# Startup order of a four-layer GNN kernel: table additions first, table parts and weight split inside the first step, statistics behind the last message, three idle products

## What is computed

```python
def _gine_layer(x, src, dst, edge_attr, eps, We, be, W1, b1, gamma, beta, W2, b2):
    e = edge_attr @ We + be                       # edge_attr: one weight w per edge
    m = jax.nn.relu(x[src] + e)
    agg = jax.ops.segment_sum(m, dst, num_segments=x.shape[0])
    h = ((1.0 + eps) * x + agg) @ W1 + b1
    mu = jnp.mean(h, axis=0)
    var = jnp.mean(jnp.square(h - mu), axis=0)
    h = (h - mu) * jax.lax.rsqrt(var + BN_EPS) * gamma + beta
    h = jax.nn.relu(h)
    return jax.nn.relu(h @ W2 + b2)
...
x = _layernorm(x + x_after_four_layers)
```

## Time and profile before

| what | value |
|---|---|
| median of 3 runs | 1656.23 us (1652.46 to 1661.26) |
| profiled execution, its own time | 1657.55 us |
| span of its trace, first to last instruction | 1655.7 us |
| mean granted TensorE clock | 0.968 of full speed |
| gathers of layer 0 from the table | 272, from 32.95 to 371.57 us |
| first gather of layer 1 | 427.21 us |

### The profile page before, as it was taken

One profiled execution on the slowest core, in us unless ns is written; L12 is line 12 of the kernel. 1 busy time (PEld: TensorE's weight loads), 2 busy tenths in 40 slices (PEclk: granted clock), 3 DMA queues, 4 the chain that ended last, 5 costly groups with the idle time before them and its releaser, 6 DMA issues. The chain is left out here.

```text
span 1655.7 us, 20783 instructions
## 1 busy us (share of the span) xinstructions
PE 1413.6 (85%) x8107; PEld 856.7 (52%) x8107; DVE 1278.7 (77%) x2059; ACT 283.3 (17%) x669; POOL 1081.9 (65%) x1149
## 2 busy tenths in 40 slices
PE   4798888889788889888968888888897888899888
PEld 3364555555444555555535555555544555565563
DVE  7997888875677878787567887787667877787867
ACT  3011111116100100111610100110170100110014
POOL 6777777770577777776067777777507777777740
PEclk9999999999899999999989999999998999999999
DMA  8777777771677777777177777777617777777743
GB/s 315 218 212 211 211 211 211 211 236 54 198 210 210 211 211 211 212 210 224 57 220 212 210 210 211 211 209 211 188 69 238 210 212 211 210 210 210 211 157 127
DMA packets 109194, 330.66 MB, mean 200 GB/s; under 512 B 20794, under 2 KB 21946, under 8 KB 109092
## 3 DMA queue, kind: packets, MB, share of 16 engines
q0 software_dynamic: 91200, 298.92, 62.1%
q1 hardware_dynamic: 17892, 30.36, 5.4%
HBM read 316.40 MB, written 12.80 MB: 199 GB/s over the span
## 5 line engine op out<-in xcount | busy, mean ns | idle before, releaser
L457 POOL DMA_INDIRECT rows<-node_table,src_all x1124 | 1062.6, 945 | 508.0 <-issue 395.8
L879 DVE SCALAR_TENSOR_TENSOR rows<-We_ps,negw_all,rows 128x512 f32<-128x512 f32 x1140 | 778.4, 743 | 283.2 <-DMA rows<-node_table,src_all 281.3
L1229 PE MATMUL y_ps<-table_parts,src_onehot 128*128 128x512 f32 x2240 | 630.8, 425 | 22.1 <-DVE src_onehot L782 22.1
L1229 PEld LDWEIGHTS y_ps<-table_parts,src_onehot 128*128 128x128 f32 x2240 | 421.3, 199 | 268.0 <-issue 165.6
L1187 PE MATMUL pair_ps<-rows,onehot 128*32 128x512 f32 x2504 | 347.8, 622 | 202.9 <-DVE rows L879 202.5
L1187 PEld LDWEIGHTS pair_ps<-rows,onehot 128*32 128x32 f32 x2504 | 51.5, 108 | 327.7 <-DVE rows L879 214.6
L782 DVE TENSOR_TENSOR src_onehot<-y_ps,src_bc 128x1280 fp32r<-128x1280 f32 x112 | 165.7, 1482 | 1.2 <-issue 1.2
L571 ACT COPY pair_sb<-pair_ps 128x512 f32<-128x512 f32 x80 | 47.0, 587 | 655.8 <-PE pair_ps L1187 655.8
L1278 PEld LDWEIGHTS h_ps<-uT,W_sb 128*128 128x128 f32 x1184 | 136.4, 193 | 31.3 <-issue 31.0
L1278 PE MATMUL h_ps<-uT,W_sb 128*128 128x128 f32 x1184 | 143.5, 279 | 0.0
L1332 PE MATMUL y_ps<-rows,hT 128*128 128x512 f32 x288 | 124.6, 593 | 1.5 <-ACT hT L652 1.5
(11 more groups left out here) (118 smaller groups left out, 646.2 us busy)
## 6 DMA issues: line engine op xcount, KB each, us to landing
rows<-node_table,src_all POOLq DMA_INDIRECT x1124, 3.7
node_table<-rows SPq DMA_DIRECT2D x29, 256.0 KB
x_now<-x_pad SPq DMA_DIRECT2D x10, 512.0 KB, 7.7
W_sb<-W SPq DMA_DIRECT2D x4, 1024.0 KB, 5.5
rows<-W SPq DMA_DIRECT2D x4, 1024.0 KB, 8.4
out<-rows SPq DMA_DIRECT2D x8, 256.0 KB
node_table<-rows SPq DMA_DIRECT2D x8, 224.0 KB
be_bc<-be SPq DMA_DIRECT2D x5, 256.0 KB, 7.9
```

The lines of the kernel that those rows point to most:

```text
L457: nc.gpsimd.indirect_dma_start(rows[:, slot, :], None, source, bass.IndirectOffsetOnAxis(places[:, t:t + 1], 0)).then_inc(landed[q], 16)
L879: last = nc.vector.scalar_tensor_tensor(rows[:, slot, :], We_of, negw_all[:, t:t + 1], row, ALU.mult, ALU.max)
L1229: last = nc.tensor.matmul(y_ps[k % 2][:, :], src_onehot[:, k % 2, b, :], table_parts[:, part, b, :], start=(part, b) == PRODUCTS[0], stop= ...
```

## The change

- VectorE's ten additions of be (L851) stand directly behind `negw_all`. The split of the weights, the one-hots and placement of block 0 and the ten `lo_part` stand behind the messages of quad 0 of layer 0's first step; the first two source one-hots behind quads 1 and 2; `keep_w(0)` behind quad 3.
- ScalarE copies the weight parts and sums of block 0 inside the first step. TensorE makes all eight spreads of source indices ahead of the layers, sums the weights behind quad 0 and places them in quad 1, and the forty products of the first two gathered tiles begin at place 0 and not before the first step.
- The columns of source indices are stored by tile and parity of the block: seven small copies for five.
- In a layer's last step the eight statistics instructions stand behind quad 7, not behind quad 6.
- `GAP`, the number of idle products at each of the two places at a layer's end, is 3 for 4.

POOL's instructions and waits are as they were, and SP's too.

```diff
-    GAP = 4
+    GAP = 3
...
-        shares, done = {}, -2
+        shares, done = {}, -2 if l else -1
...
             for m in range(3):
                 keep_spread(m)
-            act.wait_ge(w_parts_ready, 1)
-            move_parts(0, 0)
-            move_parts(0, 1)
             for k in range(BLOCKS):
                 act.wait_ge(staged, k + 1)
                 hi_part(k)
-                if k == 1:
-                    copy_w(0)
-                elif k + 2 < SPREADS:
-                    keep_spread(k + 2 + (k == 0))
+                if k + 3 < SPREADS:
+                    keep_spread(k + 3)
...
+                        else:
+                            act.wait_ge(w_parts_ready, 1)
+                            move_parts(0, 0)
+                            move_parts(0, 1)
+                            copy_w(0)
...
-            for m, q in enumerate(pe_quads(L - 1, 0)):
-                tile = FULL[q][-1][1]
-                nc.vector.tensor_copy(src_cols[:, m:3 * (BLOCKS - 1):3], src_all[:, tile:T - LAST:STEP])
-            for m, q in enumerate(pe_quads(L - 1, BLOCKS - 1)):
-                t, k = STEP * (BLOCKS - 1) + FINAL[q][-1][1], 3 * (BLOCKS - 1) + m
-                nc.vector.tensor_copy(src_cols[:, k:k + 1], src_all[:, t:t + 1])
+            for _, group in itertools.groupby(BY_TILE, key=lambda place: place[:2]):
+                (tile, _, i, q), steps = (places := list(group))[0], len(places)
+                k, t = COLUMNS[i, q], STEP * i + tile
+                nc.vector.tensor_copy(src_cols[:, k:k + steps], src_all[:, t:t + 2 * STEP * (steps - 1) + 1:2 * STEP])
...
-            left = negw_all
-            for k in range(3):
...
-            dve.wait_ge(consts_ready, 1)
-            w_onehots(0)
-            make_place(0)
 
             dve.wait_ge(be_loaded, 16)
             for k, b in enumerate(ORDER):
                 dve.wait_ge(x_loaded[b // 2], 16)
                 nc.vector.tensor_tensor(table_stage(b), x_now[:, b, :], be_bc[:, :], ALU.add).then_inc(staged, 1)
-                if k:
-                    lo_part(dve, nc.vector, k - 1, 0, lo_ready)
-            lo_part(dve, nc.vector, BLOCKS - 1, 0, lo_ready)
-            then_wait(keep_w(0))
-            nc.vector.tensor_scalar(w_sum[:, 0:1], w_sum[:, 0:1], ok[:, 0:1], None, ALU.mult).then_inc(w_sum_ready, 1)
 
             dve.wait_ge(staged, BLOCKS)
             dve.wait_ge(We_ready, 1)
             dve.sem_inc(params_free, 3)
+
+            def first_parts():
+
+                for k in range(BLOCKS):
+                    lo_part(dve, nc.vector, k, 0, lo_ready)
...
-                        if q == 3 and l == 0 and 0 < i:
+                        if q == 0 and l == 0 and i == 0:
+                            first_parts()
+                            split_w()
+                            w_onehots(0)
+                            make_place(0)
+                        if q == 1 and l == 0 and i == 0:
+                            dve.wait_ge(src_bc_ready, SPREADS)
+                            make_src_onehot(l, 0)
+                        if q == 2 and l == 0 and i == 0:
+                            make_src_onehot(l, 1)
+                        if q == 3 and l == 0:
                             keep_w(i).then_inc(w_sum_ready, 1)
...
-                        if q == 6 and i == BLOCKS - 1:
+                        if q == 7 and i == BLOCKS - 1:
                             dve.wait_ge(h_copied, n + 1)
                             kept_stats(i)
                             late_stats(BLOCKS, GUARD + (BLOCKS - 2) * P, GUARD - MARGIN + (BLOCKS - 1) * P)
...
-                make_src_onehot(l, 0)
-                make_src_onehot(l, 1)
+                    make_src_onehot(l, 0)
+                    make_src_onehot(l, 1)
...
-            sum_w(0)
-            place_w(0)
-            for m in range(4, SPREADS):
-                spread_src(m)
-
...
+                    if q == 0 and l == 0 and i == 0:
+                        sum_w(0)
+                    if q == 1 and l == 0:
+                        place_w(i)
```

More of the change, by code:

```diff
@@ L1 @@
+import itertools
 import numpy as np
@@ L93, in gnn_layers @@
     PE_TILES = [[(i, q) for i in range(BLOCKS) for q in pe_quads(l, i)] for l in range(L)]
-    COLUMNS = {place: k for k, place in enumerate(PE_TILES[-1])}
+    BY_TILE = sorted((STEPS[i][q][-1][1], i % 2, i, q) for i, q in PE_TILES[-1])
+    COLUMNS = {(i, q): k for k, (_, _, i, q) in enumerate(BY_TILE)}
     assert all(place in COLUMNS for tiles in PE_TILES for place in tiles)
@@ L791, in make_place @@
                                         ALU.is_equal).then_inc(place_ready, 1)
-            for m, q in enumerate(pe_quads(L - 1, 0)):
-                tile = FULL[q][-1][1]
-                nc.vector.tensor_copy(src_cols[:, m:3 * (BLOCKS - 1):3], src_all[:, tile:T - LAST:STEP])
-            for m, q in enumerate(pe_quads(L - 1, BLOCKS - 1)):
-                t, k = STEP * (BLOCKS - 1) + FINAL[q][-1][1], 3 * (BLOCKS - 1) + m
-                nc.vector.tensor_copy(src_cols[:, k:k + 1], src_all[:, t:t + 1])
+            for _, group in itertools.groupby(BY_TILE, key=lambda place: place[:2]):
+                (tile, _, i, q), steps = (places := list(group))[0], len(places)
+                k, t = COLUMNS[i, q], STEP * i + tile
+                nc.vector.tensor_copy(src_cols[:, k:k + steps], src_all[:, t:t + 2 * STEP * (steps - 1) + 1:2 * STEP])
+                assert [place[2] for place in places] == list(range(i, i + 2 * steps, 2))
             nc.vector.tensor_scalar(ident[:, :], cols[:, 0:P], part[:, 0:1], None,
@@ L819, in _ @@
             then_wait(nc.vector.tensor_tensor(target[:, :], target[:, :], starts[:, 0:T_PAD:PAIR], ALU.subtract))
-            dve.wait_ge(w_loaded, 16)
-            then_wait(nc.vector.tensor_scalar(negw_all[:, :], w_all[:, :], -1.0, None, ALU.mult))
-            dve.sem_inc(negw_ready, 1)
-            left = negw_all
-            for k in range(3):
[L827 to L831, removed]
             def w_onehots(b):
@@ L842, in keep_w @@
                 return nc.vector.tensor_reduce(w_sum[:, b:b + 1], w_sum_ps, mybir.AxisListType.X, ALU.add)
-            dve.wait_ge(consts_ready, 1)
-            w_onehots(0)
-            make_place(0)
+            dve.wait_ge(w_loaded, 16)
+            then_wait(nc.vector.tensor_scalar(negw_all[:, :], w_all[:, :], -1.0, None, ALU.mult))
+            dve.sem_inc(negw_ready, 1)
             dve.wait_ge(be_loaded, 16)
@@ L860, in _, with split_w @@
             dve.sem_inc(params_free, 3)
+            def first_parts():
+                for k in range(BLOCKS):
+                    lo_part(dve, nc.vector, k, 0, lo_ready)
+            def split_w():
+                left = negw_all
+                for k in range(3):
+                    then_wait(nc.vector.tensor_copy(w_parts[:, 0:T_PAD, k], left[:, :]))
+                    if k < 2:
+                        then_wait(nc.vector.tensor_tensor(rest[:, :], left[:, :], w_parts[:, 0:T_PAD, k], ALU.subtract))
+                        left = rest
+                dve.sem_inc(w_parts_ready, 1)
             def messages(q, l, i):
@@ L957, in edge_step @@
                             late_stats(BLOCKS, GUARD + (BLOCKS - 2) * P, GUARD - MARGIN + (BLOCKS - 1) * P)
-            dve.wait_ge(src_bc_ready, SPREADS)
             dve.wait_ge(cleared, 1)
             dve.wait_ge(flag_ready, 1)
-            dve.wait_ge(w_sum_ready, 1)
             slow = dve.value_load(flag[0:1, 0:1], min_val=0, max_val=1)
@@ L1001, in slow_edges @@
                 dve.sem_inc(quad_summed[7], BLOCKS)
+                if l == 0:
+                    first_parts()
+                    dve.wait_ge(src_bc_ready, SPREADS)
+                    make_src_onehot(l, 0)
                 dve.wait_ge(lo_ready, BLOCKS * (l + 1))
@@ L1004, in slow_edges @@
                     dve.wait_ge(landed[q], landed_count(q, 0, 0))
-                if l == 0:
-                    make_src_onehot(l, 0)
                 dve.wait_ge(table_written, MORE_WRITES * l + WRITES)
@@ L1138, in spread_src @@
                 last.then_inc(src_spread, 1)
-            for m in range(4):
+            for m in range(SPREADS):
                 spread_src(m)
@@ L1204, in edge_step @@
                             add_first_pair(n - 1, i - 1)
-                        if q == 1 and l == 0:
-                            place_w(i)
                         if q == (1 if final else 2):
@@ L1293, in edges @@
             def edges(l):
+                if l == 0:
+                    pe.wait_ge(src_bc_ready, SPREADS)
                 gather_share(l, -1)
```

## The result

The changed kernel takes 1660.68 us in the median of 20 runs (1657.45 to 1664.93); the kernel before took 1656.35 us beside it (20 runs, 1652.46 to 1662.86). The ratio is 1.0026 [1.0017, 1.0036], so it is slower by 4.3 us, with 2.8 to 6.0 us as the interval. The profiled execution took 1660.66 us, its span 1658.9 us. The forecast was 1661.6 us.

A forecast was written before the change was run, and what follows sets the result against it. POOL's unbroken gathers were taken to pace each layer. Start +6.3, statistics −0.6 and idle products −0.3 us on the profiled 1657.55 us gave 1662.95 us, +5.4; on the median 1656.2 us, 1661.6 us, range 1655.0 to 1667.0 us.

The forecast's parts named there:

- POOL paces layer 0, its start counts one for one: Layer 0's table gathers: 271 spacings without a wait, so the layer's end moves one for one with POOL's first gather.
- Rival 3: Layer 0: the later POOL start is absorbed, the 6.3 us shrink to about 0, about 1655.3 us; chance 10%.
- The start term: Startup of layer 0: table parts behind quad 0's messages make POOL start at 39.3 us, not 32.95, +6.3 us.
- wake: POOL's delay from the last table part to its first table gather, taken as 0.9 us.
- x's landing: Startup: the last load of x, issued at 6.2 us, lands 17.0 us later, at 23.2 us as before.
- Rival 2: SP's queue, 12 to 24 us: writes share it with x, which lands about 4 us later, 1665.6 us; chance 14%.
- The table complete at best 1.3 us earlier: Startup: earlier additions bring the table writes forward at most about 1.3 us; parameter loads may take that back.
- Rival 1: POOL's start: the writes decide, not the table parts, start moves −1.3 us, 1654.0 us; chance 6%.
- The work moved into the first step: Layer 0's first step: weight split, one-hots and placement ahead of later messages, covered by POOL's distance to the slots, nothing.
- Statistics: Layer ends: eight instructions behind quad 7 save TensorE's wait for VectorE at layer 2's end, 0 to −0.6 us, taken −0.6.
- Idle products: Layer ends, eight places: three instead of four; ACT's copy decides, so 0.04 us each, −0.3 us (bounds 0 to −1.5).
- The sum: Whole kernel: +6.3 − 0.6 − 0.3 on the profiled execution, +5.4 us, median 1661.6 us.

The follow-up runs named there:

- the chip of the long time: Not an edit: groups of runs in which every kernel, the one before too, took about 1970 us at a mean granted TensorE clock of 0.88 to 0.89.
- parts first: Changed kernel with the ten table parts put back directly behind the ten additions, ahead of quad 0's messages: 1654.28 us, ratio 0.9996; 1964.54 us in the slow group.
- parts behind quad 1: Changed kernel with the ten table parts behind quad 1's messages instead of quad 0's: 1670.54 us (5 runs), ratio 1.0093 to the kernel before.
- loads late: Kernel with the table parts back behind the additions, parameter loads released only behind those parts: 1654.38 us, ratio 0.9997; 1965.08 us in the slow group.
- tail edits: Kernel before with only statistics behind quad 7 and three idle products: 1654.93 us, ratio 0.9990; 1966.76 us in the slow group.
- quad 7 from x: Kernel with the table parts back behind the additions, plus quad 7's three gathers of layer 0's first step taken from x: 1653.12 us, ratio 0.9980.
- both strong tests: Slow-group runs holding back parameter loads: released behind the early table parts, 1965.08 us; SP waiting for all writes, with quad 7 from x, 1966.35 us.

## Why the prediction was right, point by point

- **POOL paces layer 0, its start counts one for one.** Right. 271 spacings of 0.3 us in the changed kernel too; starts of 32.11, 38.23 and 47.14 us gave last gathers of 370.90, 377.01 and 385.89 us. Rival 3 (absorbed, 1655.3 us) falls with it. On the chip of the long time a part was absorbed: 0.6 to 0.7 us of each microsecond reached layer 0's last gather.
- **The start term, +6.3 us, measured +5.28 us.** The mechanism and the order were right, the length of each step too: the flag and waits 1.45 us (forecast 1.4), one-hots to parts 5.75 us (5.8), parts 6.10 us (6.1), wake 0.84 us (0.9). The one term that was off is x's landing: forecast 23.2 us, measured 22.17 us. The last load was issued at 5.34 for 6.20 us and took 16.8 for 17.0 us. I had kept the issue time, since SP's instructions are the same; it moved all the same. A hit within 1 us is partly luck here: in kernels whose x loads are the same instructions x landed anywhere from 21.17 to 24.36 us.
- **Rival 2, the writes delay x (1665.6 us).** Falls: x landed earlier, not later. In the kernels where the additions stand first x lands at 22.17, 21.17, 21.62 and 21.91 us (the changed kernel, parts first, parts behind quad 1, loads late); in those where they alternate with the parts at 23.16, 23.06, 23.20 and 24.36 us (before, tail edits, statistics, `GAP`). But the kernel with quad 7 from x, where the additions stand first too and whose extra gathers come later, has 24.24 us, inside the other set. So the order of the additions isn't shown to be the reason, and scatter between executions may be. Where x landed early SP's queue had moved more between 8 and 21 us (2.78 and 2.77 MB in the changed kernel and with the parts first; 2.54 MB before and 2.59 MB with quad 7 from x) and the gathers' queue less (2.36 and 2.38 MB for 2.55 and 2.52 MB). Why the split differed is open. No run moved the additions and nothing else.
- **The table complete at best 1.3 us earlier, with the loads perhaps taking it back.** The last write landed at 32.46 us for 32.69 us, 0.2 us earlier, so nearly nothing came of it. The reason I had offered, the parameter loads, falls: they took nothing in both strong tests. Between x's last landing and the last write's lie 10.3, 10.7, 10.6 and 11.1 us in the changed kernel, parts first, loads late and quad 7, whatever follows the writes, and 9.5 us before. My bound divided the left bytes by the full rate; the windows point to an end that one or two late engines set. This step had no part in the sum, since the other gate is 5 us later.
- **Rival 1, the writes decide (1654.0 us).** Not so in the changed kernel, where the parts release POOL. With the parts put first it is what happens: the writes release POOL, 0.84 us earlier than before (forecast 1.3 us), and the time is 1654.28 us.
- **The work moved into the first step, at nothing.** Right: no wait of POOL appears, and the kernel with only the parts put back is level with before.
- **Statistics, −0.6 us.** Open. The times give 0.9995 [0.9981, 1.0008], −3.1 to +1.3 us; the layer ends scatter by 3 to 5 us.
- **Idle products, −0.3 us.** The wrong term: by the rows it is −0.85 us. I read that ACT's copy decides, because the weight load started right behind it. But `close_block` started 0.24 us behind the copy with four idle products and 0.05 us with three: the last idle product decided, up to the copy's bound. The value was inside the bounds I had given (0 to −1.5 us).
- **The sum.** With the measured terms it would be +5.3 − 0.6 − 0.85, about +3.9 us, against 4.3 us [2.8 to 6.0]. The forecast, +5.4 us, was 1.1 us above the measured: 1.0 us too much at the start and 0.55 us too little at the idle products, and the −0.4 us left can't be told from scatter.

## What to carry to other kernels

Look for the engine whose instructions follow each other without a single wait in a long loop: it needn't be the busiest (here it has 65%, TensorE 84%). While that holds, a delay of its start comes out at the end undiminished, and work may stand ahead of its gate only if it ends before the other gate does. The parts ended 1.4 us ahead of the last write when they stood early and 4.9 us behind it when they stood late; the writes that they made way for gained 0.2 us. When a transfer must be complete, look for its last landing and don't work it out from bytes and rate.

## What the runs showed of the hardware

- **A transfer can be late while the DMA engines are nearly idle.** With a share of 0.08 in 33 to 34.9 us a write of the table landed at 34.91 us, and with 0.06 in 31 to 32.2 us one landed at 32.26 us. That one or two engines hold it is read from the share; the trace doesn't name them. Holding back the loads behind the writes didn't hasten it (10.4 for 10.0 us from x's landing on one chip).
- **VectorE's semaphore instruction runs ahead of its queued work.** The release that stands behind ten parts in the program (24 to 30 us) let SP's load go at 26.50 us, with five parts still to start. On the chip of the long time, where the parts ran to 33.4 us, it came at 32.45 us, with one still to start, so the lead is no fixed number. Where something is to wait for the end of work, the increment has to hang on the last instruction.
- **POOL's wake depends on the gate.** It is 0.84 us from the last part's end (37.39 us) to the gather (38.23 us), the 0.93 us of the earlier trace rows within 0.1 us, but 0.26 us from the last write's landing to the gather (32.69 to 32.95 us before, 31.85 to 32.11 us with the parts first).
- **x's landing moves by 1 to 3 us** between kernels whose loads are the same instructions: 21.17 us with the parts first, 24.24 us with quad 7 from x, though their gathers up to then are the same. The cause is open.
- **One kernel, two chips:** 1654.28 us at a mean granted clock of 0.973 and 1964.54 us at 0.887. With the longer time POOL waits for TensorE and no longer paces the layer, so the same edit can have another worth: tail and start edits have to be measured where the mechanism holds. That the clock is the whole reason for the longer time isn't shown.
